# Moving the transposes and casts of the next-but-one group ahead, and the positive part of the second expert-order iteration from ACT to DVE

## The reference

```python
for _ in range(2):                                   # ITERS
    ctx = concatenate([integrated, v])               # v is 0 in the first iteration
    shared_ctrl = gelu(ctx @ shared_w1 + b1) @ shared_w2 + b2
    x_sh, v_sh  = _inl(shared_ctrl, integrated, v, mu)
    ctrl = experts(ctx of each (token, chosen expert) pair)      # top 2 of 8
    x_r, v_r = _inl(ctrl, x_e, v_e, mu)              # then weighted and summed over the 2
    halt = sigmoid(gelu(integrated @ halt_w1) @ halt_w2)
    integrated += halt * (sw * x_sh + (1 - sw) * x_r - integrated)   # v likewise
out = layernorm(x + x_in + integration_weight * refine(integrated))

def _inl(ctrl, xs, vs, mu):
    a, b, g = split(ctrl, 3)
    v_next = sigmoid(a) * vs - softplus(b) * (xs - mu)
    return xs + 0.1 * sigmoid(g) * v_next, v_next
```

## Time and profile before

| | |
|---|---|
| median of 3 runs | 1635.64 us (1633.97 to 1637.22) |
| the profiled execution | 1632.6 us |
| its span, first to last instruction | 1630.6 us |
| busy over the span | PE 1047.4, DVE 994.4, ACT 842.0, POOL 706.4 us |
| stretch B (816 to 1018 us) | 202 us: PE busy 109.94, DVE 130.74, ACT 138.98, POOL 84.43; granted clock of PE 0.80 |
| stretch S2 (1062 to 1235 us) | 173 us: PE 101.50, DVE 135.45, ACT 104.20, POOL 99.30; clock 0.81 |
| stretch D (1235 to 1436 us) | 201 us: PE 137.58, DVE 107.90, ACT 150.74, POOL 118.09; clock 0.86 |

### The profile page before, as it was taken

How to read it: one execution, slowest core, us unless ns; L and a number is a source line. 1 busy time by engine, 2 the same in 40 slices (tenths; PEclk the granted TensorE clock), 3 DMA queues, 4 the chain that set the end, 5 groups by cost and what they waited for, 6 DMA issues and landing times.

```text
span 1630.6 us, 21701 instructions
## 1 busy us (share of the span) xinstructions
PE 1047.4 (64%) x6930; PEld 649.0 (40%) x6930; DVE 994.4 (61%) x1951; ACT 842.0 (52%) x1303; POOL 706.4 (43%) x692
## 2 busy tenths in 40 slices
PE   4777988789888835642165553465547666643777
PEld 2333544445445413320044442233345555532444
DVE  1665566575666424766657775699765455543787
ACT  1134445444454613445457776265566777761554
POOL 6112223132231436017724444766447665546661
PEclk9668989899899976776578887787888888876978
DMA  4957283562834039502234443754314333314342
GB/s 77 154 74 112 39 124 65 81 109 54 124 72 60 15 88 281 176 16 98 95 105 156 156 156 119 242 185 144 109 42 134 105 110 116 91 39 145 113 121 81
DMA packets 151755, 178.84 MB, mean 110 GB/s; under 512 B 33207, under 2 KB 127826, under 8 KB 151517
## 3 DMA queue, kind: packets, MB, share of 16 engines
q1 hardware_dynamic: 134624, 124.85, 33.9%
q0 software_dynamic: 17024, 52.58, 10.8%
HBM read 100.25 MB, written 76.87 MB: 109 GB/s over the span
## 4 chain that ended last, share of the span: by engine, by line
DVE 26%; PE 15%; ACT 8%; issue 7%; POOL 5%; DMA 2%; SPq 0%; DVEq 0%; ACTq 0%; POOLq 0%
DVE e_xT L1575 6%; PE exp_ps L2076 3%; ACT ct L1457 3%; PE exp_ps L2078 3%; PE exp_ps L2077 3%; DVE ct L1755 2%; DVE rb L1757 2%; DVE rb L1759 2%; DVE ct L1736 2%; ACT g L1425 2%; DVE rb L1774 2%; POOL xg L1365 1%; PE exp_ps L2037 1%; ACT h_hl L1426 1%; DVE xs L1896 1%
## 5 line engine op out<-in xcount | busy, mean ns | idle before, releaser
L499 ACT ACTIVATE probs<-att_ps 128x512 f32<-128x512 f32 x320 | 175.7, 609 | 169.9 <-PE att_ps L739 168.9
L561 DVE TENSOR_REDUCE neg_max<-att_ps 128x1 f32<-128x512 f32 (+3 forms) x448 | 217.2, 533 | 73.0 <-PE att_ps L730 71.4
L2076 PE MATMUL exp_ps<-e_xT,w 128*128 128x128 f16 x432 | 123.7, 291 | 143.6 <-DVE e_xT L1575 143.6
L729 PE MATMUL att_ps<-k_stack,q_stack 96*128 96x512 bf16 (+3 forms) x512 | 162.9, 359 | 70.3 <-DVE neg_max L561 32.0
L1310 POOL TENSOR_TENSOR rb<-rb,ct 128x1024 f32<-128x1024 f32 x44 | 103.1, 2344 | 240.1 <-ACT ct L1477 240.0
L406 POOL TENSOR_TENSOR wait_carrier<-wait_carrier 128x1 f32<-128x1 f32 x64 | 12.3, 193 | 295.6 <-ACT probs L499 295.6
L1411 ACT CAST e_xT<-exp_ps 128x512 f16<-128x512 f32 x172 | 92.1, 609 | 89.7 <-PE exp_ps L1965 89.7
L739 PE MATMUL att_ps<-q_stack,k_stack 98*128 98x512 bf16 (+3 forms) x512 | 125.1, 318 | 7.7 <-DMA q_stack<-max_parts 5.5
L730 PE MATMUL att_ps<-mask_q,identb 128*128 128x128 bf16 x512 | 126.1, 252 | 0.0
L2077 PE MATMUL exp_ps<-e_xT,w 128*128 128x128 f16 x432 | 124.1, 292 | 0.0
L2078 PE MATMUL exp_ps<-e_xT,w 128*128 128x128 f16 x432 | 124.1, 292 | 0.0
(11 more groups left out here) (269 smaller groups left out, 3051.0 us busy)
## 6 DMA issues: line engine op xcount, KB each, us to landing
rs_dram<-rb SPq DMA_DIRECT2D x18, 1024.0 KB, 4.9
parts_dram<-parts SPq DMA_DIRECT2D x48, 256.0 KB, 2.7
q_stack<-parts_dram SPq DMA_DIRECT2D x96, 128.0 KB, 6.3
k_stack<-parts_dram SPq DMA_DIRECT2D x96, 128.0 KB, 9.7
xs_dram<-zeros SPq DMA_DIRECT2D x18, 520.0 KB, 9.8
xg<-xs_dram SPq DMA_DIRECT2D x18, 520.0 KB, 6.0
rs_dram<-rb SPq DMA_DIRECT2D x18, 512.0 KB, 3.9
x_in<-in_L_attn_encodings SPq DMA_DIRECT2D x8, 512.0 KB, 10.3
```

The source lines that it names most:

```text
L499: nc.scalar.activation(probs[:, pair % 4, u, :], src, ACT.Exp).then_inc(free, 1)
L561: return v.tensor_reduce(out, scores, AX.X, ALU.max, negate=True)
L729: t_.matmul(out, stationary, moving, start=True, stop=False)
L2076: t_.matmul(o, hi, xT[:, 0, c, tok], start=(c == 0), stop=False)
```

## The change

Three orders change, and one piece of work moves.

- In both loops PE turns n+2 before control(n), ACT casts n+2 before tanhs(n), and DVE takes the lows of n+2 right after copy and subtraction of n+1.
- In D the positive part goes from ACT (L1470) to DVE (`relus`), behind the lows; with it the wait for the store of the group two before goes from ACT to DVE.
- In D the update of n-1, which stood ahead of absolute(n), stands behind it (in the first round of D still ahead of the positive part).

```diff
@@ ACT, tanhs @@
                 if n >= 2:
                     act.wait_ge(ew_done, n - 2 + 1)
+                if n >= 2 and is_shared(n):
                     if is_shared(n - 2):
                         act.wait_ge(acc_done, shared_before(n - 2) + 1)
                     else:
...
                     else:
                         raw = slot_ps(u)[:, 0:CTRL]
                         last = s.activation(ct[:, par, i, :], raw, ACT.Tanh, scale=0.5)
+                        if not is_shared(n):
+                            last.then_inc(tanh_slot[u % 2], 1)
+                            continue
@@ ACT, loop @@
                     if n + 1 < end:
                         hidden(n + 1)
-                    tanhs(n)
                     if n + 2 < end:
                         turned(n + 2)
+                    tanhs(n)
@@ DVE, relus @@
+            def slot_tanhs(u):
+                if u < uses(W_S2):
+                    return u // 2 - W_B + 1
+                return QUADS + (u - uses(W_D)) // 2 + 1
...
-                if n - 2 >= W_B:
+                if n - 2 >= W_B and not is_shared(n - 2):
                     dve.wait_ge(rs_stored[par], 16 * (stores_before(n - 2, par) + 1))
...
+                    if it_of(n) == 1:
+                        m = rb[:, par, 2 * i:2 * i + 2, D:]
+                        b = slot_ps(u).rearrange("p (t n) -> p t n", t=2)[:, :, 0:D]
+                    else:
+                        m, b = rb[:, par, i, D:], slot_ps(u)[:, D:2 * D]
+                    v.tensor_scalar(m, b, 0.0, None, ALU.max).then_inc(ctrl_freed[u % 2], 1)
@@ DVE, loop of B @@
                 if q + 1 < QUADS:
                     hidden1(q + 1)
+                if q + 2 < QUADS:
+                    turned1(q + 2)
                 relus(W_B + q)
                 absolute(W_B + q)
                 if q:
                     first_velocity(W_B + q - 1)
-                if q + 2 < QUADS:
-                    turned1(q + 2)
@@ DVE, loop of S2 and D @@
-                if n > W_S2:
-                    update2(n - 1)
-                absolute(n)
                 if n + 2 < EWS:
                     turned2(n + 2)
+                if n >= W_D + 1:
+                    relus(n)
+                    absolute(n)
+                    update2(n - 1)
+                else:
+                    if n > W_S2:
+                        update2(n - 1)
+                    if n == W_D:
+                        relus(n)
+                    absolute(n)
@@ PE, loops @@
-                    control(n, h_hl[:, n % 2], h_h1[:, n % 2], here)
                     if W_S2 <= n + 1 < W_D and n + 1 < end:
                         halt_logits(n + 1 - W_S2)
                     if n + 2 < end:
                         turn_stage(n + 2)
+                    control(n, h_hl[:, n % 2], h_h1[:, n % 2], here)
```

More of the change, by code:

```diff
@@ L1733, in absolute @@
                 b = (ct[:, par, :, D:2 * D] if it_of(n) == 2 else ct[:, par, :, 0:D]).bitcast(U32)
-                if not W_B <= n < W_S2:
-                    dve.wait_ge(tanh_done, n + 1 - (QUADS if n >= W_S2 else 0))
+                if is_shared(n):
+                    dve.wait_ge(tanh_done, shared_before(n) + 1)
                 v.tensor_scalar(b, b, 0x7FFFFFFF, None, ALU.bitwise_and).then_inc(abs_done, 1)
+            def slot_tanhs(u):
+                if u < uses(W_S2):
+                    return u // 2 - W_B + 1
+                return QUADS + (u - uses(W_D)) // 2 + 1
             def relus(n):
                 par = n % 2
-                if n - 2 >= W_B:
+                if n - 2 >= W_B and not is_shared(n - 2):
                     dve.wait_ge(rs_stored[par], 16 * (stores_before(n - 2, par) + 1))
+                if is_shared(n - 2):
+                    dve.wait_ge(acc_done, shared_before(n - 2) + 1)
                 for u in range(uses(n), uses(n + 1)):
                     i = u - uses(n)
[L1745 to L1748, removed]
+                    dve.wait_ge(tanh_slot[u % 2], slot_tanhs(u))
+                    if it_of(n) == 1:
[4 more added lines that the diff above has]
+                    v.tensor_scalar(m, b, 0.0, None, ALU.max).then_inc(ctrl_freed[u % 2], 1)
             def velocity(n, vel):
```

## The result

The changed kernel takes 1664.31 us (median of 4 runs, 1657.49 to 1668.87); the kernel before took 1636.43 beside it (4 runs, 1633.97 to 1639.72). The ratio is 1.0192, with a 95% interval of 1.0133 to 1.0252: slower, by 1.3 to 2.5%. Its profiled execution took 1660.77 us with a span of 1658.9, 28.3 us longer than the span of before.

A forecast was written before the change was run, and what follows sets the result against it. No engine is busy throughout; D was taken as a serial ring of lows, hidden, gelu, copy, update, absolute. D +21.6, B -2, S2 0 make +20, on 1632.6 plus 3: 1655 us; range 1617 to 1677, likeliest case 1640 to 1676.

The forecast's parts named there:

- What the change does to D: D: update and copy held off by POOL's products, rounds 15.8 us instead of 14.36, +21.6 us over 15 rounds.
- the upper bound of 16.6: D: round length in us if PE stands at 1.2 GHz when tile 2 comes, 1.1 to 1.2 us more.
- the sum's 15.5: D: round length in us from adding the steps from one absolute to the next, hold-offs included.
- B: Loop B: a ring through POOL replaces one through PE, rounds 10.1 to 10.3 us against 10.26; -2 us, bounds -4 to +1.
- S2: Stretch S2: late first control, more hold-offs and one shorter round together 0 us, bounds -6 to +6.
- the round without combination: S2: the round of 20.50 us in which nothing is combined becomes 16.5, -4 us.
- the late first control: S2: first control stands behind a turn that waits for a combination, 0 to 4 us, taken as 3.
- the five combining rounds: S2: products start among the combining instructions and hold them off, less the halt gate wait, +1.5 us in all.
- DVE keeps its turn: Rival: copy and subtraction go ahead of the waiting second product, D 13.3 us a round, 1618 us; chance 0.12.
- Not held off at all: Rival: update and subtraction never held off, D 11.7 and B about 8.0 us, 1560 us; chance 0.06.
- Nothing gained or lost: Rival: D's held-off time is about one product shorter every second round, D near 14.4 us, 1633 to 1638; chance 0.08.
- much slower: Rival: S2's control late in all rounds, 7 x 3 us more, 1676 to 1690 us; chance 0.08.

The follow-up runs named there:

- Experiment 3: Changed kernel with POOL's second product left out in D: 1626.18 us.
- experiment 5: Changed kernel with PE's register loads of group n+2 moved between the tiles of control(n) in D: 1664.85 us.
- experiment 7: Changed kernel with the lows of n+2 ahead of copy and subtraction of n+1 in B alone: 1666.98 us, 8.87 us a round of B.
- experiment 9: Changed kernel with 12 extra matrix products before tile 2 in D and the early register loads between them: 1664.77 us.
- experiment 4: Changed kernel with 28 extra matrix products per D group, keeping PE at work while it waits for tile 2: 1667.22 us.
- experiment 6: Changed kernel with D's positive part back on ACT and PE's register loads of n+2 moved between control(n)'s tiles: 1636.33 us.
- experiment 2: Changed kernel with the update of n-1 in D put back ahead of the positive part and absolute(n): 1708.95 us.
- experiment 10: Changed kernel with D's positive part on ACT, early register loads, and the store waited for by DVE's third update instruction: 1604.25 us, ratio 0.9814.

## Why the prediction was right

**What the change does to D: right, and the size short.** Every step stands in the timeline: the third update instruction at 3.26 us (forecast about 3.3), the copy at 2.43 (2 to 2.4), each behind a product, the lows, the first positive part only then, and no wait for the store. Experiment 3 shows the copy's hold-off on the lap, experiment 5 that PE's own list does not set it. The mis-sized step is "I take 15.8, nearer to the lower of these two because only part of the rounds will meet it": all 14 rounds met PE at 1.2 GHz at tile 3 and 11 of them at both tiles, after waits of 4.2 us on the mean (forecast some 6), and a round took 16.37, near the upper bound of 16.6. Two errors partly cancelled: the clock costs 2 x 0.62 = 1.2 us a round by the spacing of the pairs, not 0.3, and so the rest is some 15.1, below the sum's 15.5. That sum added whole durations, while DVE's rows overlap (the absolute lasts 0.68 us and the next starts 0.60 after it). Over D the term was +21.6 and measured +28.7, of which the last two rounds, counted at 0, gave 2.0. The lock that the Trainium skill states ("SBUF — State Buffer", section "SBUF: two separate sides"), by which subtraction and update are held off as well, agrees with the trace: 2.75 us for a subtraction in B, 3.26 for an update in D.

**B: right in kind, too small.** The subtraction at 2.75 us (forecast about 2.7) and the lap through POOL are as forecast, and experiment 7 confirms the lap. The round is 9.84 and not 10.1 to 10.3, again by rows that overlap; -9.3 instead of -2, beyond the bound of -4.

**S2: the failed term.** 0 was taken, bounds -6 to +6, and it came to +9.3 up to D's first absolute. Right were the round without combination (20.50 to 16.21 us, forecast 16.5) and the late first control (+4.7, forecast 3, at most 4). Wrong were the five combining rounds, +1.5 in all by the forecast and some 1.3 each by the trace: the two combining instructions lose 2.0 and 2.1 us (1.1 and 2.1 before), as counted, and the wait for the halt gate is gone, as counted; but the lows now wait for casts, which I had not counted (0.60 us in the S2 rows above, then 0.16 before each of the next two). In S2 the lows stand right behind the combination for which the transposes of the same group wait (5.72 us in the same rows), so transposes and casts can't be done by then. And D's first absolute comes 3.2 us later after S2's last (19.98 instead of 16.81 us), for which there was no term. That is the positive part's doing: the distance is 19.95 to 19.98 us in every run with it on DVE and 15.46 to 15.47 in every run with it on ACT. The five rounds' 1.3 us come with the transposes ahead (21.95 to 22.36 us a round in all runs that have them); no run took the waits of the lows away.

**The sum and the rivals.** +20 became +28.3 of span; the time of 1664.31 lies in the range and in the forecast's own part of it (1640 to 1676), 9 us above the point. That it is so near is partly luck: the errors of D (+7.1) and B (-7.3) cancelled, and S2's 9.3 remained. "DVE keeps its turn" fell: the copy did not pass the waiting second product in D. "Not held off at all" fell with 3.26 and 2.43 us. "Nothing gained or lost" fell, and "much slower" too, for S2's control was late in the first round alone. The price of the clock rests on spacings and on single rounds (experiment 9); the attempt to take it away in every round (experiment 4) ran into the second lap.

## What to carry to other kernels

A change of three parts should be costed and run as its parts: here two groups ahead alone gives 0.9911, and handing a short piece of work from one engine to a less busy one, with the update moved behind it, turned that into 1.0192, because the piece stood behind a long list on its new engine and another engine waited for it. When a lap is shortened, look for the next lap of nearly the same length before counting the gain: experiment 4 lost nearly all of its gain to one, experiment 6 all of it. And instructions of DVE and POOL that both work in SBUF should be placed so that what lies beside POOL reads PSUM, as in experiment 7.

## What the runs showed of the hardware

- Reading four numbers into PE's registers takes 2.46 us on its list, 0.64 each, and shows in the profile only as "issue" before the next product; placed between tiles that wait anyway it was free (experiment 5).
- A POOL product that starts while an instruction of DVE holds it off shows the wait in its own length: 3.12 and 3.21 us in the changed kernel, 2.35 and 2.36 in experiment 2, where no update stands beside it.
- PE's granted clock was 0.76 in D of the changed kernel, where PE waits 4.2 us on the mean for the positive part in every round, and 0.96 in 180 us of D of experiment 10, where it waits less than half as long (15 waits of 1.4 us on the mean and one of 6.4).
